# Down weights of the narrow experts in two 4 KB runs per partition, in a one-core graph network and mixture-of-experts kernel

## The chip, the cores and the metric

The kernel runs on one core of one Trainium2 chip. Its time is the device time of one execution in microseconds (us); the number that counts is the median of several. Weights lie in the chip's memory (HBM) and are copied by 16 DMA engines into SBUF, a memory of 128 partitions; TensorE (PE in the profile) multiplies from SBUF into PSUM; ScalarE (ACT) and VectorE (DVE) work between PSUM and SBUF; GpSimd (POOL) issues the gathers and scatters, SyncE (SP) the weight loads.

## The reference, cut to what matters

Two parts follow each other. The first is a graph layer on 625 rows of 512 (a segment sum over 10,625 edges, two matrix products with batch norms); it ends in x. The second is a mixture of 64 routed and 2 shared experts on the same 625 rows:

```python
x = layernorm(x)                                 # 625 x 512, one row per token
for e in range(2):                               # shared experts, all tokens
    shared += silu(x @ sWg[e]) * (x @ sWu[e]) @ sWd[e]
probs = softmax(x @ Wr)                          # 625 x 64
top_w, top_i = top_k(probs, 6)                   # six experts per token, renormalised
for e in range(64):                              # routed experts
    routed += silu(x @ Wg[e]) * (x @ Wu[e]) @ Wd[e] * gate[:, e:e+1]
out = x + shared + routed
```

Everything is float32. Each of Wg[e], Wu[e] and Wd[e] is 512 x 512, so 1 MB, and an expert has 3 MB. The kernel does not run all tokens through every expert: it gathers the rows that chose an expert, computes on those, and adds the results back by index.

## The kernel before

Up to about 200 us the graph layer runs. Then come the 64 experts, one after the other, in an order sorted by how many rows chose them (the first six are taken as they come). `CAPS` gives each position j in that order its number of slots: 96 for the first 22 positions, 64 (`BIG`) for the other 42. A position with 96 slots does its products in two pieces, 64 + 32; one with 64 slots has the first piece only. Rows beyond the slots would go through a loop at the end, whose count is read from the routing.

**Weights.** SP walks through a list `items`: gate and up weights of position j, then the down weights of position j-1. Load i goes to buffer i modulo 13 (`ring`, which in the profile has the names ring, w and ring_x, since five of the buffers share their place with earlier tensors). Before load i SP waits until the product that used the load 13 places earlier is done, reads the expert's number and issues a DMA of 1 MB. The gate and up weights are laid out "(p k)": partition p holds rows 4p to 4p+3, which are 8 KB in one piece of memory. The down weights are laid out "(k p)": partition p holds rows p, 128+p, 256+p and 384+p, which are four pieces of 2 KB.

**Products.** `tiled` (L1274) makes a product of a 64-slot position with 8 weight tiles: four slices k of the 512 rows, and for each the left and the right half of the 512 columns. The left half of the columns goes to PSUM partitions 0 to 63 and the right half to partitions 64 to 127, 256 columns each. So partition (h, token) of the gate product, column c, is feature 256h + c. `silu` (L578, ACT) turns bank 0 of PSUM into `hs`; `mult` (L941, DVE) multiplies it by the gate value and by the up product in bank 1. `h_transpose` (L1290) turns the two blocks of 128 columns of `hs`; block b then has, at partition p, features 128b + p of both halves, that is rows 256h + 128b + p of the down weights, which is slice k = 2h + b. `h_copy` moves it to `hTj`, `down` (L1298) multiplies with the down weights, `y_copy` moves the result to `ysb`, and GpSimd adds it to `out_tab` in HBM by index.

**Order on TensorE**, written out by hand, for position j: gate product of j; transposes of `hs` of j-1; transposes of the gathered rows of j+1; the small index product of j+4; up product of j; at every second position from 15 to 61 one piece of a shared expert (`unit`); down product of j-1. ACT does silu of j, the copy of `hTj` of j-1, the copy of `xT` of j+1, its part of the shared piece, and `y_copy` of j-1. DVE does the indices of j+4, the one-hot of j+6, `mult` of j and its part of the shared piece.

**Tail.** When the last scatters have landed, SP loads the two halves of `out_tab`, DVE adds them to x, and SP writes the result out.

Of the kernel before, what the change touches and what calls it, by code (L numbers as in the profile page):

```python
# [16 lines left out]
ALU = mybir.AluOpType  # L17
ACT = mybir.ActivationFunctionType
# [3 lines left out]
def gnn_moe_kernel(nc, x_in, src_in, dst_in, eps_in, W1, b1, g1, be1, W2, b2, g2, be2,  # L22
# [19 lines left out]
    BIG, SMALL = 64, 32  # L42
    CAP = BIG + SMALL
    AW = D // 2
# [5 lines left out]
    NR = 13  # L50
# [4 lines left out]
    CAPS = [CAP] * NBIG + [BIG] * (E - NBIG)  # L55
# [5 lines left out]
    with ctx:  # L61
# [129 lines left out]
        hs = [rWin.place(f"hs{i}", [128, HW], f32) for i in range(2)]  # L191
# [10 lines left out]
        ring = [rOh.place(f"ring{i}", [128, KD, 512], f32) for i in range(8)]  # L202
# [20 lines left out]
        ps = ctx.enter_context(nc.psum_tensor("ps", [128, 8, 512], f32))  # L223
# [4 lines left out]
        def sem(name):  # L228
            return ctx.enter_context(nc.semaphore(name))
# [6 lines left out]
        s_ring = [sem(f"ring_in{i}") for i in range(NR)]  # L236
# [26 lines left out]
        s_silu, s_mul, s_hc, s_y = (sem(n) for n in ("silu_done", "h_done", "hT_copied", "y_ready"))  # L263
# [14 lines left out]
        shared.append(sWd.rearrange("e (k p) n -> e p k n", p=128))  # L278
        experts = [w.rearrange("e (p k) n -> e p k n", p=128) for w in (Wg, Wu)]
        experts.append(Wd.rearrange("e (k p) n -> e p k n", p=128))  # L280

        items = []
        for j in range(E):
# [20 lines left out]
        @block.sync  # L304
        def _(sp):
            sp.dma_start(dst_i[:], dst_in.rearrange("(c p) -> c p", p=P)).then_inc(s_edges, 16)
            sp.dma_start(src_i[:], src_in.rearrange("(c p) -> c p", p=P)).then_inc(s_edges, 16)
            sp.dma_start(x_sb[:], x_in.rearrange("(t p) d -> p t d", p=P)).then_inc(s_x, 16)

            for i in range(2):  # L310
                sp.dma_start(w1[i][:], w1_of[i]).then_inc(s_w1[i], 16)
            sp.wait_ge(s_adj, T)
            for i in range(2):
                sp.dma_start(w2[i][:], w2_of[i]).then_inc(s_w2[i], 16)
            for r in range(3):
                sp.dma_start(sw[r][:], shared[r][0]).then_inc(s_sw[r], 16)
            done = (s_g, s_u, s_d)
            number = {j: j for j in range(FIXED)}
            for i, (r, j) in enumerate(items):
                if i == 8:  # L320
                    sp.wait_ge(s_z, KH)
                if i == 10:
                    sp.wait_ge(s_z, KH + KD)
                if i == 12:
                    sp.wait_ge(s_acc, 1)
                    sp.wait_ge(s_xnp, T)
                    sp.wait_ge(s_xtab, 16)
                if i >= NR:
                    r0, j0 = items[i - NR]
                    sp.wait_ge(done[r0], j0 + 1)  # L330
                if j not in number:
                    if j == FIXED:
                        sp.wait_ge(s_sorted, 1)
                    number[j] = sp.value_load(order[0:1, j:j + 1], min_val=0, max_val=E - 1)
                sp.dma_start(ring[i % NR][:], experts[r][number[j]]).then_inc(s_ring[i % NR], 16)

            sp.wait_ge(s_ov, 1)
            total = sp.value_load(ovrow[0:1, 2 * MAXOV:2 * MAXOV + 1], min_val=0, max_val=MAXOV)
            with sp.If(total > 0):
                with sp.Fori(0, total) as o:  # L340
                    e = sp.value_load(ovrow[0:1, bass.ds(o + MAXOV, 1)], min_val=0, max_val=E - 1)
                    sp.wait_ge(s_d, o + E)
                    for r in range(3):
                        sp.dma_start(ring[r][:], experts[r][e]).then_inc(s_ring[r], 16)

            sp.wait_ge(s_sy, NS * T)
            sp.wait_ge(s_scat[0], total * 16 + 8 * E)
            sp.dma_start(sums[0][:], out_tab[0][0:N, :].rearrange("(t p) d -> p t d", p=P)).then_inc(s_sum0, 16)
            sp.wait_ge(s_scat[1], 8 * E)
            for t in range(T):  # L350
                sp.dma_start(sums[1][:, t, :], out_tab[1][t * P:(t + 1) * P, :]).then_inc(s_sum1[t], 16)  # L351
            for t in range(T):
                sp.wait_ge(s_fin, t + 1)
                sp.dma_start(out[t * P:(t + 1) * P, :], x_sb[:, t, :]).then_inc(s_out, 16)
            sp.wait_ge(s_out, 16 * T)
# [90 lines left out]
        def _(act):  # L446
            sc = nc.scalar
# [68 lines left out]
            for d in range(KD):  # L516
                i = KH + d
# [60 lines left out]
            def silu(j, h, wide):  # L578
                act.wait_ge(s_g, j + 1)
                if not isinstance(j, int) or j >= 2:  # L580
                    act.wait_ge(s_th, j - 1)
                sc.activation(hs[h][:, 0:wide], ps[:, 0, 0:wide], ACT.Silu).then_inc(s_silu, 1)  # L582

            def h_copy(j, wide):
                act.wait_ge(s_th, j + 1)
# [22 lines left out]
            for j in range(E):  # L608
                silu(j, j % 2, WIDE[j])
                if j >= 1:  # L610
                    h_copy(j - 1, WIDE[j - 1])
                if j + 1 < E:
                    x_copy(j + 1, (j + 1) % 2, CAPS[j + 1])
                if j in unit_at:
                    unit(*unit_at[j])
                if j >= 1:
                    y_copy(j - 1, (j - 1) % 2, (j - 1) // 2, CAPS[j - 1])
# [4 lines left out]
            with act.If(total > 0):  # L622
                with act.Fori(0, total) as o:
                    x_copy(o + E, 0, CAP)
                    silu(o + E, 0, AW)
                    h_copy(o + E, AW)
                    y_copy(o + E, 0, o + E // 2, BIG)
# [3 lines left out]
        def _(dve):  # L631
            v = nc.vector
# [308 lines left out]
            def mult(j, h, ga, gb, wide):  # L941
                dve.wait_ge(s_silu, j + 1)
                dve.wait_ge(s_u, j + 1)
                last = v.scalar_tensor_tensor(hs[h][:, 0:AW], hs[h][:, 0:AW], ga, ps[:, 1, 0:AW], ALU.mult, ALU.mult)  # L944
                if wide > AW:
                    last = v.scalar_tensor_tensor(hs[h][:, AW:wide], hs[h][:, AW:wide], gb, ps[:, 1, AW:wide],
                                                  ALU.mult, ALU.mult)
                last.then_inc(s_mul, 1)
# [30 lines left out]
            for j in range(E):  # L979
                if j + AHEAD < E:  # L980
                    indices(j + AHEAD)
                if j + AHEAD + 2 < E:
                    slot_onehot(j + AHEAD + 2)
                mult(j, j % 2, gates[:, j, 0:1], gates[:, j, 1:2], WIDE[j])
                if j in unit_at:
                    unit(*unit_at[j])
                if j == 3:
                    extra_tiles()
                if j == 5:
                    extra_rows()  # L990
            total = dve.value_load(ovrow[0:1, 2 * MAXOV:2 * MAXOV + 1], min_val=0, max_val=MAXOV)
            with dve.If(total > 0):
                with dve.Fori(0, total) as o:
                    e = dve.value_load(ovrow[0:1, bass.ds(o, 1)], min_val=0, max_val=E - 1)
# [422 lines left out]
```

## Time and profile before

| | us |
|---|---|
| median of 3 runs | 872.74 |
| lowest, highest | 871.55, 873.14 |
| the profiled execution's own time | 871.14 |
| its span in the profile | 869.4 |
| TensorE busy | 778.0 (89%) |
| VectorE busy | 275.7 (32%) |
| ScalarE busy | 200.0 (23%) |
| GpSimd busy | 175.5 (20%) |

The span is what the profile shows from its first to its last instruction. The share of the DMA engines and the rate in GB/s are given by stretch of the span. A weight load is one instruction of SP, and its bytes move as packets on queue q1; the gathers and scatters go through q0. Of 71,518 packets 54,542 are under 8 KB. SP's instructions stand as SPq: their duration is the time until the DMA is handed over, not until it has landed.

### The profile page before, as it was taken

The page shows a single profiled execution, that of the slowest core. Times are in us where ns is not written, and L with a number is a line of the kernel's source. Part 1 is how long each engine was busy: PE and PEld are TensorE (multiplying, and loading weights), DVE is VectorE, ACT ScalarE, POOL GpSimd, SP SyncE. Part 2 cuts the span into 40 slices and gives each one's busy share as a digit, 9 for nine tenths or more (in the row PEclk, how much of TensorE's full clock was granted, in tenths as well). Part 3 has the DMA queues.
Part 4 walks back from the last instruction along what each step waited for, and adds up shares of the span by engine and source line. Part 5 has one row for each costly group of instructions (what it writes and reads, how often), then busy time and mean ns, then how long its engine had stood idle before and what let it go on. Part 6 is the DMA issues. An engine that isn't in the chain of part 4 may idle for free. (4 is left out here: it accounts for less than half of the span.)

```text
span 869.4 us, 18070 instructions
## 1 busy us (share of the span) xinstructions
PE 778.0 (89%) x7224; PEld 523.2 (60%) x7224; DVE 275.7 (32%) x833; ACT 200.0 (23%) x506; POOL 175.5 (20%) x155
## 2 busy tenths in 40 slices
PE   0789999959798999999999999999999999999920
PEld 0466877747566676666666666656666666555510
DVE  7875054366625223222111222221221121221002
ACT  0020132223022333232323222212222222122200
POOL 4000000000322233322111323222222232222110
PEclk9999999967699999999999999999999999999975
DMA  6200882032299999998988999999999999999943
GB/s 220 92 1 1 305 324 97 1 105 99 85 318 302 338 365 373 359 359 282 302 286 278 372 374 381 366 373 380 378 366 374 374 382 374 373 375 383 393 123 121
DMA packets 71518, 242.43 MB, mean 279 GB/s; under 512 B 7749, under 2 KB 7913, under 8 KB 54542
## 3 DMA queue, kind: packets, MB, share of 16 engines
q1 hardware_dynamic: 57892, 213.88, 66.0%
q0 software_dynamic: 12512, 24.12, 11.2%
q10 hardware_dynamic: 1034, 3.30, 1.0%
q8 instruction: 58, 0.95, 0.4%
q14 instruction: 22, 0.18, 0.1%
HBM read 225.72 MB, written 15.54 MB: 278 GB/s over the span
## 5 line engine op out<-in xcount | busy, mean ns | idle before, releaser
L417 POOL DMA_INDIRECT out_tab<-ysb,idx_sb x64 | 92.2, 1440 | 370.6 <-ACT ysb L593 219.2
L1278 PE MATMUL ps<-ring,xT 128*64 128x256 f32 x1296 | 158.4, 387 | 2.9 <-DMA ring<-in_L_ffn_Wu 1.1
L1278 PEld LDWEIGHTS ps<-ring,xT 128*64 128x64 f32 x1296 | 89.6, 138 | 46.6 <-issue 8.0
L899 DVE TENSOR_REDUCE gates<-ps 128x1 f32<-128x3 f32 (+1 forms) x64 | 10.3, 161 | 286.9 <-PE ps L1215 286.9
L592 ACT ACTIVATE ysb<-ps 64x256 f32<-64x256 f32 x64 | 24.1, 377 | 306.7 <-PE ps L1278 184.9
L406 POOL DMA_INDIRECT xg<-x_tab,idx_sb x64 | 70.9, 1108 | 111.7 <-DVE idx_sb L905 65.3
L1278 PE MATMUL ps<-ring,hTj 128*64 128x256 f32 x624 | 75.2, 383 | 0.0
L1278 PE MATMUL ps<-w,xT 128*64 128x256 f32 x608 | 73.4, 383 | 1.3 <-DMA w<-in_L_ffn_Wu 1.3
L861 DVE TENSOR_TENSOR onehot<-iotaAB,slotv 125x640 bf16<-125x640 f32 (+1 forms) x64 | 66.9, 1045 | 0.7
L1278 PEld LDWEIGHTS ps<-ring,hTj 128*64 128x64 f32 x624 | 42.6, 137 | 29.3 <-issue 10.4
L944 DVE SCALAR_TENSOR_TENSOR hs<-hs,gates,ps 128x256 f32<-128x256 f32 x64 | 30.7, 480 | 86.1 <-PE ps L1278 58.3
L1278 PEld LDWEIGHTS ps<-w,xT 128*64 128x64 f32 x608 | 41.7, 137 | 21.2 <-issue 3.0
L1069 PE MATMUL ps<-oh,win 125*125 x220 | 44.9, 338 | 6.9 <-DVE win L719 5.2
L1270 PE MATMUL ps<-ident,xg 64*128 64x64 f32 (+1 forms) x256 | 43.0, 289 | 0.5 <-DVE gid L845 0.5
L582 ACT ACTIVATE hs<-ps 128x256 f32<-128x256 f32 (+1 forms) x64 | 26.9, 420 | 71.3 <-PE ps L1278 40.0
L1069 PEld LDWEIGHTS ps<-oh,win 125*125 x220 | 29.0, 145 | 23.2 <-issue 13.9
L1242 PE MATMUL ps<-xnT,sw 128*128 128x312 f32 (+1 forms) x128 | 40.1, 458 | 0.4 <-ACT lg L536 0.4
L1270 PEld LDWEIGHTS ps<-ident,xg 64*128 64x128 f32 (+1 forms) x256 | 35.7, 210 | 7.8 <-issue 7.0
L1278 PE MATMUL ps<-w,hTj 128*64 128x256 f32 x320 | 38.7, 384 | 1.4 <-ACT hTj L586 1.0
L396 POOL DMA_DIRECT2D x_tab<-xn x1 | 1.7, 1669 | 178.9 <-DVE xn L743 178.9
L1250 PE MATMUL ps<-xnT,sw 128*128 128x312 f32 (+1 forms) x128 | 36.6, 428 | 0.7 <-DVE hsT L957 0.7
L1261 PE MATMUL ps<-sw,hsT 128*125 128x512 f32 x80 | 37.0, 605 | 0.0
(257 smaller groups left out, 923.2 us busy)
## 6 DMA issues: line engine op xcount, KB each, us to landing
ring<-in_L_ffn_Wg SPq DMA_DIRECT2D x41, 1024.0 KB, 18.6
ring<-in_L_ffn_Wu SPq DMA_DIRECT2D x40, 1024.0 KB, 19.3
ring<-in_L_ffn_Wd SPq DMA_DIRECT2D x39, 1024.0 KB, 20.0
w<-in_L_ffn_Wd SPq DMA_DIRECT2D x20, 1024.0 KB, 20.3
w<-in_L_ffn_Wg SPq DMA_DIRECT2D x19, 1024.0 KB, 11.4
w<-in_L_ffn_Wu SPq DMA_DIRECT2D x19, 1024.0 KB, 19.3
ring_x<-in_L_ffn_Wu SPq DMA_DIRECT2D x5, 1024.0 KB, 14.8
ring_x<-in_L_ffn_Wd SPq DMA_DIRECT2D x5, 1024.0 KB, 18.8
```

What stands on the lines that cost most here:

```text
L406: g.indirect_dma_start(out=xg[j % NX][0:CAPS[j], :], out_offset=None, in_=x_tab, in_offset=bass.IndirectOffsetOnAxis(ap=idx_sb[0:CAPS[j], ...
L417: g.indirect_dma_start(out=out_tab[h], out_offset=bass.IndirectOffsetOnAxis(ap=idx_sb[0:CAPS[j], j:j + 1].bitcast(u32), axis=0), in_=ysb[h ...
L582: sc.activation(hs[h][:, 0:wide], ps[:, 0, 0:wide], ACT.Silu).then_inc(s_silu, 1)
L592: sc.activation(ysb[h][0:BIG, 0:AW], ps[0:BIG, 3, 0:AW], ACT.Copy)
L861: v.tensor_tensor(onehot[e % 2][:].rearrange("p t a c -> p t (a c)")[:, :, 0:n], iotaAB[0:P, :, :].rearrange("p a c -> p (a c)")[:, 0:n].u ...
L944: last = v.scalar_tensor_tensor(hs[h][:, 0:AW], hs[h][:, 0:AW], ga, ps[:, 1, 0:AW], ALU.mult, ALU.mult)
L1069: t_.matmul(o, win[:, i * U + u, :], oh[:, c, c0:c1], start=False, stop=False)
L1242: last = t_.matmul(ps[:, 5, 0:PART[h]], sw[0][:, k, f * 128:(f + 1) * 128], xnT[:, k, c0:c0 + PART[h]], start=(k == 0), stop=(k == KD - 1))
L1250: last = t_.matmul(ps[:, 6, 0:PART[h]], sw[1][:, k, f * 128:(f + 1) * 128], xnT[:, k, c0:c0 + PART[h]], start=(k == 0), stop=(k == KD - 1))
L1261: last = t_.matmul(ps[0:P, 5, :], hsT[:, k, t * P:(t + 1) * P], sw[2][:, k, :], start=(k == 0), stop=(k == KD - 1))
L1270: last = t_.transpose(ps[:, 4, k * rows:(k + 1) * rows], xg[h][0:rows, :].rearrange("p (c k) -> p k c", k=KD)[:, k, :], ident[0:rows, 0:rows])
L1278: last = t_.matmul(ps[h * BIG:(h + 1) * BIG, bank, 0:AW], big(k), w[:, k, h * AW:(h + 1) * AW], start=(k == 0), stop=(k == KD - 1))
```

## The change

It concerns the 42 positions with 64 slots, and the loop for rows beyond the slots. Partition p of their down weights now holds rows 2p and 2p+1 of the upper 256 rows and rows 256+2p and 256+2p+1 of the lower ones: two pieces of 4 KB. For the transposed `hs` to fit, block b must hold the features 256h + 2p + b. So silu and the multiplication read PSUM in steps of two columns: first the even columns, which go to the first 128 columns of `hs`, then the odd ones, which go to the second 128. The bytes loaded, the transposes, the products and all waits are as before. The 22 positions with 96 slots keep the old layout throughout.

```diff
         experts.append(Wd.rearrange("e (k p) n -> e p k n", p=128))
+        down_pairs = Wd.rearrange("e (h p b) n -> e p h b n", h=2, b=2)
...
-                sp.dma_start(ring[i % NR][:], experts[r][number[j]]).then_inc(s_ring[i % NR], 16)
+                if r == 2 and CAPS[j] == BIG:
+                    sp.dma_start(ring[i % NR][:].rearrange("p (h b) n -> p h b n", h=2),
+                                 down_pairs[number[j]]).then_inc(s_ring[i % NR], 16)
+                else:
+                    sp.dma_start(ring[i % NR][:], experts[r][number[j]]).then_inc(s_ring[i % NR], 16)
...
-                    for r in range(3):
+                    for r in range(2):
                         sp.dma_start(ring[r][:], experts[r][e]).then_inc(s_ring[r], 16)
+                    sp.dma_start(ring[2][:].rearrange("p (h b) n -> p h b n", h=2), down_pairs[e]).then_inc(s_ring[2], 16)
...
-                sc.activation(hs[h][:, 0:wide], ps[:, 0, 0:wide], ACT.Silu).then_inc(s_silu, 1)
+                o, i = hs[h][:, 0:wide], ps[:, 0, 0:wide]
+                if wide == AW:
+                    o, i = o.rearrange("p (b c) -> p b c", b=2), i.rearrange("p (c b) -> p b c", b=2)
+                sc.activation(o, i, ACT.Silu).then_inc(s_silu, 1)
...
-                last = v.scalar_tensor_tensor(hs[h][:, 0:AW], hs[h][:, 0:AW], ga, ps[:, 1, 0:AW], ALU.mult, ALU.mult)
+                o, u = hs[h][:, 0:AW], ps[:, 1, 0:AW]
+                if wide == AW:
+                    o, u = o.rearrange("p (b c) -> p b c", b=2), u.rearrange("p (c b) -> p b c", b=2)
+                last = v.scalar_tensor_tensor(o, o, ga, u, ALU.mult, ALU.mult)
```

## Rows read from the trace of the kernel before

**Rows 1.** The page: span, and the DMA queue of the weight loads.
```profile
span 869.4 us, 18070 instructions
q1 hardware_dynamic: 57892, 213.88, 66.0%
```

**Rows 2.** Windows: stretch, length; busy by engine (count); clock, DMA share, GB/s.
```profile
400.00:500.00 100.00, 100.00 (x1203) 66.86 (x1200) 19.35 (x58) 27.48 (x78) 22.33 (x19) 1.00 0.93 311
600.00:700.00 100.00, 100.00 (x758) 65.07 (x758) 20.50 (x62) 23.30 (x61) 26.02 (x22) 1.00 1.03 374
740.00:785.00 45.00, 43.46 (x315) 25.38 (x311) 9.30 (x27) 9.42 (x25) 11.67 (x10) 1.00 1.04 377
785.00:828.00 43.00, 40.76 (x301) 24.27 (x297) 4.25 (x11) 9.05 (x24) 9.00 (x7) 1.00 1.03 383
```

**Rows 3.** Waits of the SP queue, 500 to 600, then 600 to 700 us.
```profile
SPq L334 <- PE ps L1278: 30.5, 11, 5.9
...
SPq L335 <- PE ps L1278: 2.0, 3, 1.1
```

**Rows 4.** Waits of TensorE, 700 to 835 us: us in total, times, longest.
```profile
PE ps L1278 <- DMA w<-in_L_ffn_Wu: 1.3, 2, 0.9
PE ps L1278 <- DMA ring<-in_L_ffn_Wu: 1.1, 2, 0.6
PE ps L1278 <- DMA ring<-in_L_ffn_Wg: 1.1, 3, 0.6
PE ps L1278 <- ACT hTj L586: 1.0, 1, 1.0
PE ps L1278 <- DMA w<-in_L_ffn_Wd: 0.5, 1, 0.5
```

**Rows 5.** DMA issues in 500 to 800 us: the down weights.
```profile
ring<-in_L_ffn_Wd SPq DMA_DIRECT2D x20, 1024.0 KB, 22.5
...
w<-in_L_ffn_Wd SPq DMA_DIRECT2D x9, 1024.0 KB, 22.8
...
ring_x<-in_L_ffn_Wd SPq DMA_DIRECT2D x3, 1024.0 KB, 21.8
```

**Rows 6.** Windows in which the weight queue runs alone (columns as in rows 2).
```profile
98.00:102.00 4.00, 3.23 (x29) 3.07 (x29) 0.00 (x0) 0.59 (x1) 0.00 (x0) 1.00 1.02 428
107.00:114.00 7.00, 7.00 (x27) 5.06 (x28) 1.29 (x5) 0.99 (x2) 0.00 (x0) 1.00 1.02 419
103.00:105.00 2.00, 2.00 (x21) 2.00 (x20) 0.00 (x0) 0.00 (x0) 0.00 (x0) 1.00 1.04 391
124.00:125.00 1.00, 1.00 (x5) 0.71 (x4) 0.00 (x0) 0.79 (x2) 0.00 (x0) 1.00 1.03 383
```

**Rows 7.** Timeline, one 64-slot position: start, us, instruction.
```profile
642.79 0.38 ACT L582 ACTIVATE hs<-ps 128x256 f32<-128x256 f32 x1 [0.96 <-PE ps L1278]
643.15 0.38 ACT L586 ACTIVATE hTj<-ps 128x256 f32<-128x256 f32 x1
...
645.65 1.90 PE L1278 MATMUL ps<-w,hTj 128*64 128x256 f32 x16
645.94 0.48 DVE L944 SCALAR_TENSOR_TENSOR hs<-hs,gates,ps 128x256 f32<-128x256 f32 x1 [0.81 <-PE ps L1278]
...
649.21 0.44 PE L1295 MATMUL ps<-ident,hs 128*128 128x128 f32 x2
```

**Rows 8.** Timeline of the last position and its scatter.
```profile
827.91 0.48 DVE L944 SCALAR_TENSOR_TENSOR hs<-hs,gates,ps 128x256 f32<-128x256 f32 x1 [5.91 <-PE ps L1278]
828.29 1.95 PE L1278 MATMUL ps<-w,hTj 128*64 128x256 f32 x16 [0.49 <-DMA w<-in_L_ffn_Wd]
...
830.17 0.44 PE L1295 MATMUL ps<-ident,hs 128*128 128x128 f32 x2
...
836.62 1.42 POOL L417 DMA_INDIRECT out_tab<-ysb,idx_sb  x1 [3.35 <-issue]
```

**Rows 9.** Groups of DVE, 195 to 225 us: a strided and a contiguous operation of 320 elements.
```profile
L844 DVE CAST gid<-lg 125x320 bf16<-125x320 f32 x1 | 1.1, 1051 | 0.0
...
L837 DVE TENSOR_TENSOR gate<-gate,rsum 125x320 f32<-125x320 f32 x1 | 0.5, 491 | 0.0
```

## The prediction

> **What bounds the kernel now.** I read the windows first, then the waits of SP and of TensorE, then the timeline at the end. The windows show two full resources at once. From 600 to 700 us TensorE is busy for all 100 us at the full granted clock, 2.4 GHz, and the DMA engines are full too: share 1.03, 374 GB/s [rows 2]. A busy TensorE can still be fed late, so the waits decide. Between 500 and 600 us SP, which issues the weight loads, still waits for TensorE to give buffers back: 30.5 us at one line alone. Between 600 and 700 it waits 2.0 us at its largest row [rows 3]. So the ring is full up to about 600 us and TensorE sets the pace; afterwards SP only waits for its queue and DMA sets it, while TensorE lives on what has already landed. About 740 us that is used up: in 740 to 785 TensorE is idle for 45.00 - 43.46 = 1.54 us, in 785 to 828 for 43.00 - 40.76 = 2.24 us [rows 2]. The waits name the cause: 1.3 + 1.1 + 1.1 + 0.5 = 4.0 us from 700 to 835 are for weights to land (gate, up and once down weights), and 1.0 us is for a copy on ACT [rows 4]. The two windows give 3.78 of it, and the rest lies just behind 828 us. No earlier product of the 64-slot positions waits on a weight load, so 4.0 us is all that faster loads can give back on TensorE.
>
> What follows TensorE is a chain in series: last product, `y_copy`, the last scatter at 836.62 [rows 8], its landing, the load of the sums, the output. It shifts with TensorE's end and the change touches none of it.
>
> **The down loads.** Each of the 42 moves the same 1.0486 MB, as 256 runs of 4 KB and not 512 of 2 KB. The price of a run's length can be read where the weight queue runs alone, at 93 to 126 us. The order of issue is known from the code (two loads of W2, shared gate, up, down, two pairs of gate and up, a down, a pair, a down), and at about 2.5 us each the stretches can be told apart. The layouts with 8 KB runs go at 428 and 419 GB/s, those with 2 KB runs at 391 and 383 [rows 6], the DMA share being 1.02 to 1.04 in all. With 420 and 390 a load takes 2.50 and 2.69 us, 0.19 apart. No row shows 4 KB loads. If each run has a fixed cost beside its bytes, four runs per partition against one cost 0.19 us, and two against one 0.06, so the change saves 0.13 us per load. The ends are 0 (the rate beside gathers and scatters is set by something else than runs) and 0.19 (4 KB is as good as 8). I take 0.13, which lies between the two rates that the trace has.
>
> From 500 to 800 us 20 + 9 + 3 = 32 down loads are issued [rows 5], all of them for 64-slot positions. In all of that time the DMA engines are full, and what they save stays in the ring as a lead. 32 x 0.13 = 4.2 us, against 4.0 us of stalls. It also comes early enough: at the first stalls, about 745 us, some 26 loads have saved 3.4 us, and the stalls up to 785 us are 1.5. At 400 to 500 us the share is 0.93 with 311 GB/s [rows 2], the engines are not full, and I count nothing there. So all stalls on weights go: -4.0 us. It is close: at 0.09 per load instead of 0.13 the lead is 2.9 us and stalls of 1.1 us stay.
>
> The Trainium skill speaks against this term. In "DMA: Bandwidth & Descriptors", Specifications, a transfer has its full line rate from 512 B up; by that rule 2 KB runs lose nothing, the saving is 0 and the time stays at 872.7. The alone-running stretches disagree, with 391 against 419 to 428 GB/s, and I go by them; this rule gets its chance as rival 1.
>
> SP's side: the number of load instructions and their waits are the same. Fewer runs can only shorten the hand-over of a load to the queue; TensorE does not wait for SP. POOL's queue, with the gathers and scatters, is not moved, and it has the same packets. Its packets take turns with longer ones, which I estimate at under 1 us per scatter, and a scatter's buffer is needed only two positions later, over 13 us away.
>
> **The reads in steps of two.** 42 silus (0.38 us each) and 42 multiplications (0.48) read PSUM every second word [rows 7]. No row shows such a read from PSUM. From below it is free; from above stands a DVE operation with steps, 320 elements in 1051 ns against 491 without [rows 9], a factor of 2.1, so +0.4 us on silu and +0.5 on the multiplication. I take 0, since the 1051 row also writes two-byte numbers ten bytes apart and nothing here does. Either way it is covered. Behind silu on ACT stands the copy of `hTj`, which ends at 643.53; the down product that needs it starts its multiplications at 645.65, so there are about 1.9 us (PE loads its first weights about 0.2 us before). Behind `mult`, which ends at 646.42, come the transposes at 649.21: 2.8 us [rows 7]. ACT's next copy, of `xT`, would be late by what silu grew, and is needed only at the next gate product, about 3 us later. At the very end cover is thinnest: the last `mult` ends at 828.39, the transposes start at 830.17, and 0.49 us of that distance is a stall that I expect to go [rows 8]: 1.3 us of cover against 0.5. Cost 0. Once the two together exceeded their cover by x, 42 positions would pay 42x.
>
> The Trainium skill has a rule here too, in "SBUF — State Buffer", the note on cachelines: PSUM has lines of two float32 values, and a pattern that is not contiguous slows matmuls. Only ACT and DVE read PSUM here. If the same held for them and every read took twice as long, the additions of 0.38 and 0.48 us would lie under the same cover and the sum would not change.
>
> **Sum.** Profiled execution: 871.14 - 4.0 = 867.1 us (the span 869.4 becomes 865.4). The median of the runs shown lies 1.6 us above that execution, so 872.74 - 4.0 = 868.7 us. The 1.0 us wait for `hTj` stays: ACT is then at the `y_copy` of the position before, in the same order as now.
>
> **Rivals.**
> 1. *The packet length does not count in a loaded queue.* 374 to 383 GB/s with scatters in between [rows 2] is well under both lone rates, so memory or the turns with q0 may be what limits; weights on q1 have 66.0% of the engines' time over the span [rows 1], and all else would have to fill in. Then a Wd load lands when it did, and the stalls stay: 872.7. Against it: the share is above 1 in both, so the engines themselves are the full resource. Also here: the run of two rows is cut back into rows when the DMA is built, and the change does not do what it says. The 8 KB layout, whose four rows move faster than four separate rows, speaks against that. Together 0.20.
> 2. *Half of it.* The saving is about 0.07 per load, 32 x 0.07 = 2.2 us of lead, the last stalls stay: 872.7 - 2.2 = 870.5, on the edge of what can be told. 0.15.
> 3. *Slower: 4 KB runs 512 KB apart move worse than 2 KB runs 256 KB apart*, for example because the 16 engines then meet in the same part of the memory. Place: the queue from 500 us on, in the ring's lead. It decides as soon as a down load is longer at all, as TensorE already stalls at the end; every 0.1 us per load gives 32 x 0.1 = 3.2 us, so 876 us. For it speaks only that the pattern is new; against it that the 8 KB layout, with larger steps from partition to partition, is the fastest of the trace. 0.06.
> 4. *Slower: the reads outgrow their cover*, beyond 1.9 us for silu. Nothing in the rows comes near (the ends are 0.4 and 0.5). 0.02.
>
> The forecast itself has 0.57. What differs from these cases by accident of the runs is small: two medians of this kernel can be told apart at about 0.2%, 1.75 us, so faster means under 871.0 and slower over 874.5. The forecast and two thirds of rival 2 are faster: 0.57 + 0.10 = 0.67, and rounding in a small possibility of more at the tail (the last scatters meet fewer weight packets) 0.68. Same: rival 1 and the rest of rival 2, 0.25. Slower: 0.07. The range starts at 866.8, 1.9 us under the forecast, for a saving of 0.19 per load with a shorter tail, and ends at 873.0, above rival 1.
>
> **What would show it.** Right: in the changed kernel TensorE's waits for weights after 700 us are gone or under 0.5 us; q1 has some 42 x 256 = 10,752 packets fewer than 57,892 and less than 66.0% of the engines; SP waits for TensorE (buffers) beyond 600 us; the last down product ends about 4 us earlier and the tail behind it has its old length; silu and `mult` stay at 0.38 and 0.48 us. Wrong: the packets are as many as before (not done), or fewer with the share as before (rival 1); stalls that are more (rival 3); TensorE waiting for `hs` or `hTj` in mid-stage (rival 4).

## The result: 866.65 us, half a per cent faster

The changed kernel takes 866.65 us (median of 6 runs, 864.33 to 868.56); the kernel before, run beside it, 871.65 us (6 runs, 869.87 to 873.14). The ratio is 0.9942 with a 95% interval of 0.9925 to 0.9958. That is 5.0 us less where 4.0 were forecast, and the interval, 3.7 to 6.5 us, holds the forecast. The time itself lies 2 us under the forecast 868.7 and 0.15 us under the lower end of the range, 866.8.

The page of the changed kernel, beside [rows 1]:

```profile
span 866.8 us, 18070 instructions
q1 hardware_dynamic: 47140, 213.88, 65.4%
```

The weight queue has 57,892 - 47,140 = 10,752 packets fewer, as 42 loads of 256 instead of 512 give, for the same bytes. Its share is smaller: 0.660 x 869.4 = 573.8 us per engine before, 0.654 x 866.8 = 566.9 after, 6.9 us or 0.16 us per changed load. The same reading in two more executions with 4 KB runs (e1 and e2 below) gives 0.20 and 0.22, so it is good to some 0.05 us.

Windows of the changed kernel, beside [rows 2]:

```profile
600.00:700.00 100.00, 100.00 (x755) 64.96 (x753) 21.17 (x65) 23.38 (x62) 26.03 (x23) 1.00 1.03 383
740.00:785.00 45.00, 45.00 (x330) 26.36 (x332) 10.18 (x30) 10.19 (x28) 12.80 (x11) 1.00 1.03 378
785.00:825.00 40.00, 40.00 (x301) 23.69 (x299) 4.39 (x13) 9.06 (x25) 9.01 (x7) 1.00 1.01 385
```

With the DMA engines as full as before, 383 GB/s pass from 600 to 700 us instead of 374 (from 500 to 800 us it is 381 instead of 375), and TensorE has no idle time in the two stretches in which it had 1.54 and 2.24 us.

The waits of TensorE, 700 to 835 us, beside [rows 4], and one row of SP's waits from 600 to 700 us, beside [rows 3]:

```profile
PE ps L1290 <- ACT hTj L595: 1.0, 1, 1.0
PE ps L1290 <- DMA w<-in_L_ffn_Wd: 0.2, 1, 0.2
...
SPq L335 <- PE ps L1290: 14.3, 9, 2.8
```

The waits for gate and up weights are gone and one of 0.2 us for the last but one down weights is left; SP is again waiting for TensorE in a stretch in which it waited for its queue alone.

The end of the stage in the changed kernel, beside [rows 8]:

```profile
825.56 0.48 DVE L956 SCALAR_TENSOR_TENSOR hs<-hs,gates,ps 128x256 f32<-128x256 f32 x1 [5.22 <-PE ps L1290]
825.61 1.95 PE L1290 MATMUL ps<-w,hTj 128*64 128x256 f32 x16 [0.17 <-DMA w<-in_L_ffn_Wd]
827.49 0.44 PE L1307 MATMUL ps<-ident,hs 128*128 128x128 f32 x2
...
828.88 1.95 PE L1290 MATMUL ps<-w,hTj 128*64 128x256 f32 x16 [0.96 <-ACT hTj L595]
...
833.94 1.42 POOL L423 DMA_INDIRECT out_tab<-ysb,idx_sb  x1 [3.35 <-issue]
```

**Where the two profiled executions differ.** They are only 871.14 - 868.56 = 2.6 us apart. The multiplications on VectorE are a clock for the whole stage, since they start at the same rhythm in both. Here is position 11, first before, then after:

```profile
348.76 0.48 DVE L944 SCALAR_TENSOR_TENSOR hs<-hs,gates,ps 128x256 f32<-128x256 f32 x1 [0.88 <-PE ps L1283]
```

```profile
351.00 0.48 DVE L956 SCALAR_TENSOR_TENSOR hs<-hs,gates,ps 128x256 f32<-128x256 f32 x1 [0.88 <-PE ps L1295]
```

At this point the changed kernel is 2.24 us late, in work that the change does not touch. Most of it is there early. VectorE, idle before this comparison of the graph layer, starts it 1.61 us later, and the profile names no engine or transfer that it waits for. First before, then after:

```profile
22.94 3.09 DVE L719 TENSOR_TENSOR win<-iota,dcol 125x1375 int16 x2 [3.45 <-issue]
```

```profile
24.55 3.09 DVE L728 TENSOR_TENSOR win<-iota,dcol 125x1375 int16 x2 [5.05 <-issue]
```

In the twelve executions of the experiments this gap was 2.94 to 5.19 us, so it varies by itself. By 212 us some 0.5 us of the distance has come back, and another 1.2 us is added in a window in which the granted clock was 0.83 and not 0.91, before and then after:

```profile
270.00:290.00 20.00, 17.67 (x268) 12.33 (x262) 8.21 (x30) 4.62 (x12) 5.91 (x4) 0.91 0.88 297
```

```profile
270.00:290.00 20.00, 17.67 (x236) 12.21 (x234) 7.72 (x34) 5.63 (x16) 4.40 (x3) 0.83 0.83 278
```

An index product near its start begins at 271.69 before and at 272.74 after, 1.05 us later; a product near its middle begins at 281.58 and 283.82, 2.24 us later. TensorE was longer at the lower of its two levels (1.2 and 2.4 GHz). The last down product before the change starts here:

```profile
831.56 1.95 PE L1278 MATMUL ps<-w,hTj 128*64 128x256 f32 x16 [0.95 <-ACT hTj L586]
```

From position 11 to the last multiplication the rhythm gives 827.91 - 348.76 = 479.15 us before and 825.56 - 351.00 = 474.56 after, 4.59 less; to the start of the last down product 831.56 - 348.76 = 482.80 and 828.88 - 351.00 = 477.88, 4.92 less. Read so, the profile agrees with the 5.0 us of the runs. From that product to the last scatter it is 5.06 us in both, so the tail moved along unchanged.

### The profile page after: what moved, and what is told of

It is laid out like the page before. It is cut to its first block and busy times, and to the rows that moved or that the text cites. A ratio compares the mean times of both kernels' runs of the same rounds, so it can differ in the third digit from the quotient of the medians.

```text
span 866.8 us, 18070 instructions
## 1 busy us (share of the span) xinstructions
PE 777.1 (90%) x7224; PEld 522.1 (60%) x7224; DVE 275.4 (32%) x833; ACT 200.2 (23%) x506; POOL 175.6 (20%) x155
## 3 DMA queue, kind: packets, MB, share of 16 engines
q1 hardware_dynamic: 47140, 213.88, 65.4%
```

## The experiments

Each ratio is against the kernel before, run on the same chip beside it. "Rhythm" is the time from the multiplication of position 11 to that of position 63 in the profile: 479.15 us before, 474.56 after the change.

**e1: the changed kernel once more.**

> The changed kernel once more, beside the kernel before on one chip. Theory (lead in the ring: shorter down loads take away TensorE's waits for weights at the end of the expert stage): 4.6 us under before, by the starts of the multiplications on VectorE in the two traces (-2.24 us of distance at position 53, +2.35 at position 63), so a ratio of 0.9947. Rival (part of the 5.0 us measured is the graph layer's clock in the runs that happened to be drawn): the ratio comes out nearer to 1, 0.996 or more, here.

Measured: 867.41 us, ratio 0.9938 (0.9923 to 0.9954), 5.4 us less. The gain repeats, and is not smaller. Its profiled execution had 0.7 us of waits for weights, 0.2 and 0.5 us before the last up and the last but one down product, where the first one had 0.17. Its rhythm is 474.81 us, 4.34 less than before.

**e2: 4 KB runs alone; e3: stepped reads alone.** Each takes the other half of the change away:

```diff
 e2, in silu and in mult
-                if wide == AW:
-                    o, i = o.rearrange("p (b c) -> p b c", b=2), i.rearrange("p (c b) -> p b c", b=2)
 e3
-                if r == 2 and CAPS[j] == BIG:
+                if False:
```

> The 4 KB runs without the reads in steps of two (the pairing of features and weight rows is left out). Theory: the same time as e1 within 0.5 us, no wait of TensorE for gate or up weights. Rival (the stepped reads cost or bring something): it differs from e1 by over 1 us.

> The reads in steps of two on the old layout of 2 KB runs (the pairing of features and weight rows is left out). Theory: as before within 1 us, TensorE's waits for weights in the last 100 us of the stage some 4 us as before, silu 383 ns and multiplication 480 ns. Rival (the reads take part in the gain or cost): off from before by over 1.5 us.

Measured: e2 867.79 us, ratio 0.9945 (0.9930 to 0.9960), rhythm 474.56 us; e3 872.08 us, ratio 1.0000 (0.9987 to 1.0012), rhythm 479.0 us, with 1.3 us of waits at its largest row, for gate weights. Up to the intervals, of some 1.3 us each way, all of the gain is in the load and the stepped reads cost nothing. ACT and DVE took as long in the changed kernel as before, where the medians are 383 and 480 ns (operation, shortest, median and longest in ns, where the longest of ACT is the 384-column form):

```profile
L591 ACT ACTIVATE hs<-ps x64: 384/384/492, 234.7 to 823.2; 128x256 f32<-128x256 f32 x42, 128x384 f32<-128x384 f32 x22
...
L956 DVE SCALAR_TENSOR_TENSOR hs<-hs,gates,ps x64: 479/480/483, 239.7 to 825.6; 128x256 f32<-128x256 f32 x64
```

**e4: half of the down weights left out.**

```diff
-                    sp.dma_start(ring[i % NR][:].rearrange("p (h b) n -> p h b n", h=2),
-                                 down_pairs[number[j]]).then_inc(s_ring[i % NR], 16)
+                    sp.dma_start(ring[i % NR][:, 0:2, :], down_pairs[number[j]][:, 0]).then_inc(s_ring[i % NR], 16)
```

> The 64-slot positions load only the first half of their down weights (256 rows, one 4 KB run per partition; the other half is left out), 0.5 MB or 1.25 us of DMA less per position. It asks whether the changed kernel is at the floor that TensorE sets. Theory: all waits for weights are gone already but for 0.2 us, so it is at most 0.5 us under e1. Rival (DMA still limits somewhere in the changed kernel, for example before position 22 or by slowing other transfers): 2 us or more under e1.

Measured: 866.58 us, ratio 0.9935 (0.9921 to 0.9948); no wait for weights at all. Its multiplications of positions 11 and 63:

```profile
349.76 0.48 DVE L955 SCALAR_TENSOR_TENSOR hs<-hs,gates,ps 128x256 f32<-128x256 f32 x1 [0.88 <-PE ps L1294]
...
824.32 0.48 DVE L955 SCALAR_TENSOR_TENSOR hs<-hs,gates,ps 128x256 f32<-128x256 f32 x1 [5.22 <-PE ps L1289]
```

824.32 - 349.76 = 474.56 us, the rhythm of the changed kernel to the hundredth. So up to this multiplication the change reaches the floor that TensorE sets, and 4.59 us is what the waits had cost until then. Behind it a little is left. The last down product of e4 starts here:

```profile
827.25 1.95 PE L1289 MATMUL ps<-w,hTj 128*64 128x256 f32 x16 [0.96 <-ACT hTj L594]
```

That is 827.25 - 349.76 = 477.49 us after position 11, where it is 482.80 before and 477.88 after the change. In all the waits for weights had cost 5.3 us, of which the change takes away 4.9.

**e5: 8 KB runs for the down weights.** The load takes the "(p k)" view of the gate weights.

> All 64-slot positions load their down weights in one 8 KB run per partition, as gate and up (the pairing of features and weight rows is left out; the same bytes). Theory: each load is another 0.06 us shorter, but nothing waits for it any more: same time as e1 within 0.5 us. q1's share falls further, to about 65.0%, and SP waits longer for TensorE. Rival (the run length still pays): 1.5 us or more under e1.

Measured: 867.16 us, ratio 0.9947 (0.9931 to 0.9964), rhythm 474.56 us again. q1's share is 64.9%, where e1 has 65.2%, and SP waits far more for buffers: 42.5 us at its largest row from 600 to 700 us, where the changed kernel has 14.3. The loads did become shorter, and all that was left to gain from it was 0.4 us at the last products (829.11 - 351.61 = 477.50 us to the last down product).

**e6 and e7: 4 KB runs for half of the positions.**

```diff
-                if r == 2 and CAPS[j] == BIG:
+                if r == 2 and CAPS[j] == BIG and j < 43:      (e6; e7 has j >= 43)
```

> 4 KB runs for the down weights of positions 22 to 42 only, 2 KB runs for 43 to 63 (the pairing is left out for the latter). Theory: the ring carries a lead over, so time saved from about 480 us on still counts at 745 us; some 16 of these 21 loads fall in the stretch with full DMA engines, 16 x 0.13 = 2.1 us, so about 2.1 us under before (0.9976). Rival (only loads near the stalls count): as before.

> 4 KB runs for positions 43 to 63 only, 2 KB runs for 22 to 42 (the pairing is left out for those). Theory: 21 x 0.13 = 2.7 us of lead, so about 2.7 us under before (0.9969) and stalls of about 1.9 us left in TensorE's waits; at 0.16 per load 3.4 us. Rival (only loads near the stalls count): as e1, 4.6 us under before.

Measured: e6 869.01 us, ratio 0.9963 (0.9947 to 0.9979); e7 869.03 us, ratio 0.9969 (0.9953 to 0.9986). The times do not tell them apart (3.2 and 2.7 us under before by the ratios, each within 1.5), the rhythm does: e6 476.84 us, 2.3 saved; e7 475.99, 3.2 saved. e6's waits, 0.7 us each for gate and up weights and less for others, all come after 785 us, while its last 4 KB load was issued at 619.29 us, over 160 us before. So time saved early is carried along in the ring: the rival, that only late loads count, fails on both. In e7 all 21 loads lie where the engines are full, which gives a direct price. The up product of position 63, which the last multiplication follows, waits for its weights in both kernels, first before, then e7:

```profile
825.85 1.95 PE L1278 MATMUL ps<-ring,xT 128*64 128x256 f32 x16 [0.63 <-DMA ring<-in_L_ffn_Wu]
```

```profile
822.86 1.95 PE L1290 MATMUL ps<-ring,xT 128*64 128x256 f32 x16 [0.43 <-DMA ring<-in_L_ffn_Wu]
```

In the order of the list, the down weights of positions 62 and 63 come behind these up weights. So 19 of the 21 changed loads stand before them, and a down load in two runs per partition costs 3.16 / 19 = 0.17 us less than one in four (0.16 with e3's 479.0 us in place of before's rhythm). At that price e6's 2.31 us are 14 loads; I had counted 16.

**e8: gate and up weights in 2 KB runs, on the kernel before.**

> The kernel before with the gate and up weights of the 64-slot positions in four 2 KB runs instead of one of 8 KB (the pairing with the gathered rows is left out; the same bytes). It prices the run length with a large dose. Theory (each run has a fixed cost in a loaded queue too): 0.19 us more per load, 0.38 per position, over the some 36 positions with full DMA engines 13.7 us slower, and a little more since the lead is gone earlier: 884 to 889 us. Rival (in the loaded queue memory or the turns with the other queue set the rate): as before within 2 us.

Measured: 882.2 us, ratio 1.0124 (1.0099 to 1.0149), slower by 10.8 us by the ratio and 10.0 by the rhythm (489.18 us). The direction and the place are the theory's, with 4.6 us of waits at the largest row, for gate weights, but the size is three quarters of it: with the 36 positions that I had counted 10.0 / 72 = 0.14 us per load, where 0.19 was expected; e6's 14 loads of 21 would put the beginning at position 29 and give 70 loads, again 0.14. The median lies under the range I had given. DMA engines at share 1.06 moved 364 GB/s from 600 to 700 us:

```profile
600.00:700.00 100.00, 98.49 (x737) 64.24 (x735) 19.35 (x58) 23.23 (x61) 25.90 (x22) 1.00 1.06 364
```

**e9: 8 KB runs with the right pairing.** Other than in e5, nothing is left out here. To allow it, the two halves of PSUM take other columns in the gate and up products:

```diff
+                        if quads:
+                            cols = w[:, k, :].rearrange("p (g h b) -> p h g b", h=2, b=2)[:, h]
```

> 8 KB runs for the down weights with the right pairing: the gate and up products of the 64-slot positions take columns 4g, 4g+1 for one half of PSUM and 4g+2, 4g+3 for the other (the moving operand is read in pairs, 16 bytes apart), so that with the stepped reads of the change partition g holds features 4g to 4g+3 and the down weights can lie as the gate weights do. Theory (the changed kernel is at TensorE's floor): same time as e1 and e5, 867 us or ratio 0.994, if TensorE reads pairs at full pace; 16 matmuls of a product stay at 1.9 us. Rival (a read that is not contiguous slows the product): the product takes longer, and every 0.1 us of it is 84 x 0.1 = 8.4 us, so slower than before from 0.06 us on.

Measured: 873.7 us, ratio 1.0030 (1.0019 to 1.0042), about 8 us behind e1 by the two ratios. The rival wins, and the 8 KB loads are not the reason, since e5 has them without the loss. In e9 a gate and an up product take 1.98 and 2.04 us from first to last of their 16 matmuls (1.90 and 1.95 in the changed kernel), the down product behind them, with its old columns, 1.91:

```profile
644.37 1.98 PE L1292 MATMUL ps<-w,xT 128*64 128x256 f32 x16
...
647.48 2.04 PE L1292 MATMUL ps<-w,xT 128*64 128x256 f32 x16
649.34 1.91 PE L1292 MATMUL ps<-w,hTj 128*64 128x256 f32 x16
```

0.085 x 84 = 7.1 us; the rhythm grew by 481.80 - 474.56 = 7.24.

**e10 to e12: work of TensorE moved behind the last product,** to see how much lead the ring has left. One or two 3.7 us pieces of the second shared expert go there, and the first sums' buffer moves to the ring's place:

```diff
+        unit_at = {15 + 2 * i: u for i, u in enumerate(units[GAP:len(units) - TAIL])}
+        late_units = units[len(units) - TAIL:]
...
             down(E - 1, weights(2, E - 1), WIDE[E - 1])
+            for u in late_units:
+                unit(*u)
```

> The changed kernel with the last piece of the second shared expert (3.7 us of TensorE) moved behind the last down product, where TensorE is otherwise idle, and the first sums' buffer moved to the ring so that it can be loaded meanwhile. It asks how much lead the 4 KB runs leave over. Theory (e6 and e7 together saved 5.5 us of landing time where 4.6 was needed): TensorE wants 3.7 us more, 0.9 of it is there, so about 0.9 us under e1 and some 2.8 us of waits for weights are back. Rival (no DMA limit is left in the changed kernel): 3.7 us under e1.

> e9 and the moved piece together. Theory: 8 KB runs save another 0.06 us in each of some 36 loads, 2.3 us, beside the 0.9 left over: 3.2 of the 3.7 us can be had, so 863 to 864 us, ratio 0.990 to 0.991, with at most 0.6 us of waits for weights. Rival (the sums or the tail take the time back, or the pairs slow TensorE): no better than e1.

> As e11 with the last two pieces behind the last down product. Theory: the lead is used up by the first piece, so the waits for weights grow by about 3.7 us and the time is that of e11 within 1 us. Rival (TensorE alone sets the time): another 3.7 us under e11.

Measured: e10 865.62 us, ratio 0.9940 (0.9927 to 0.9953), no better than e1. Its waits for weights are back:

```profile
PE ps L1297 <- DMA ring<-in_L_ffn_Wg: 2.1, 2, 1.2
...
PE ps L1297 <- DMA w<-in_L_ffn_Wd: 0.5, 1, 0.5
PE ps L1297 <- DMA ring<-in_L_ffn_Wd: 0.4, 1, 0.4
PE ps L1297 <- DMA ring<-in_L_ffn_Wu: 0.2, 1, 0.2
```

From its position 11 (349.25 us) to its last multiplication (823.76) it is 474.51 us, although 3.7 us of TensorE's work are gone from between: the lead that the 4 KB runs leave over is nearly nothing, not the 0.9 us expected. Its up product of position 63 starts at 821.70 - 349.25 = 472.45 us, where it is 825.85 - 348.76 = 477.09 before: all the 4 KB loads together bring these weights 4.6 us earlier, not the 2.3 + 3.2 = 5.5 of e6 and e7. Where the other 0.8 us went was not separated. The changed kernel stands at both limits at once.

e11 gave 870.40 us, ratio 0.9989 (0.9976 to 1.0002), and e12 867.09 us, 0.9954 (0.9941 to 0.9967). Both times are wrong for my theory, and the rivals hold. With 8 KB runs and e9's slower products, which give DMA 7 us more, neither has a wait for weights, and each piece moved is worth its full price (rhythm of e9 481.80, of e11 478.03, of e12 474.25: 3.77 and 3.78 less). The ratios fall by 0.0041 and 0.0035, 3.6 and 3.1 us. The tail thus hides two pieces, and the slower products cost more than these bring. None of the twelve is measurably better than the change itself.

## Where the prediction was wrong, and what in it was right

The time came out under the range. The mechanism held, but two terms of the sum were off: what the stalls cost was put too low, and the starting point of 872.74 us was too high. The price per load was too low as well.


- *Which resource ends last* was right: TensorE paces the stage up to about 740 us, then it waits for weights (e4 takes just these waits away and gets the same rhythm as the change). The wait rows of the changed kernel fell to 0.2 us as I had said; in e1 they were 0.7, over the 0.5 that I had given as a sign.
- *The stalls, 4.0 us,* is the step that failed: I took the summed wait rows as "all that faster loads can give back on TensorE". Against e4 the stalls cost 4.6 us up to the last multiplication and 5.3 to the start of the last down product, and the change took 4.9 of these away (4.35 in e1's execution). A wait also breaks the overlap of one product with the next, and no wait row carries that. Before the change the down product starts at 786.18 and the gate product, which waits for weights, at 788.30:

```profile
786.18 1.90 PE L1278 MATMUL ps<-ring,hTj 128*64 128x256 f32 x16
788.30 1.95 PE L1278 MATMUL ps<-ring,xT 128*64 128x256 f32 x16 [0.23 <-DMA ring<-in_L_ffn_Wg]
```

```profile
786.52 1.90 PE L1290 MATMUL ps<-ring,hTj 128*64 128x256 f32 x16
788.25 1.90 PE L1290 MATMUL ps<-ring,xT 128*64 128x256 f32 x16
```

  The second fence is the changed kernel. From start to start it is 2.12 us with the wait and 1.73 without, 0.39 us, of which the row shows 0.23. The rest is the overlap: without the wait the gate product starts 0.17 us before the modelled end of the down product (786.52 + 1.90 = 788.42). The same comparison of starts at each of the eight waits gives 0.16 to 0.18 us beyond the row at the three gate products, 0.07 or 0.08 at the four up products and nothing at the down product. About 0.05 us more is lost at the transposes behind each gate product, and 0.15 before one up product that has no wait row at all. With 0.17 us of wait left in the changed kernel, its rows account for 3.8 of the 4.9 us, and these pieces for the other 1.1.
- *The price,* 0.13 us per load, was too low: 0.16 to 0.17 by e7, 0.16 to 0.22 by q1's share. This and the stalls go together: at 0.13 the forecast lead of 4.2 us could not have paid for the 4.9 us that came back. The lead was enough, but by e10 with next to nothing over.
- *The stepped reads cost nothing:* right, and more so than I had argued. I covered up to 0.5 us each; there was nothing to cover (e3). The rule of the Trainium skill on PSUM's lines ("SBUF — State Buffer", cachelines) speaks of matmuls; in ACT and DVE, with one step of two float32 values, no such cost is seen. e9 shows 4% on TensorE, but for a moving operand in SBUF, where the same note lets float32 step up to 16 bytes for free.
- *Rival 1,* with the Trainium skill's line rate from 512 B up ("DMA: Bandwidth & Descriptors", Specifications), is excluded: e2 has the gain with nothing changed but the runs, and e8 makes the gate and up runs 2 KB and loses 10 us at full DMA engines. *Rival 2* (half of it) saves 2.2 us, and the interval begins at 3.7. *Rivals 3 and 4* did not occur.
- *The scale,* 872.74 us, was a median of 3. The kernel before has since had medians of 871.65 (6 runs), 872.08 (17), 871.86 (26) and 870.82 (23), single runs from 867.58 to 874.06. Of the 2.05 us between forecast and result, 1.1 is this and 1.0 the gain. My range went 1.9 us below the forecast, less than these two together: its lower end took in a better price per load, but neither a lower base nor a larger sum of stalls. That three runs had a median 1.1 us high is accident, not mechanism; without it the time would have been inside the range.

**Open.** Two runs fewer per partition saved 0.17 us per load (e7), three more cost 0.14 (e8). A fixed cost per run would make these 0.17 and 0.25. The time of q1's packets did grow by about that: 0.675 x 880.5 = 594.3 us per engine in e8 against 573.8, over 84 loads 0.24 us each. Why only 0.14 of it reached the kernel's time is not shown.

## What to carry to other kernels

When two resources are full at once, ask from which point on the one that feeds is late, and read the sum of stalls as start-to-start differences of a regular instruction, not from the wait rows: here these showed 4.0 of 5.3 us. A saving per transfer then counts from the moment at which the transfers run without a gap, as long as a deep ring can carry it; beyond what the stalls cost it is worth nothing. And put a new order on the engine with slack: a stepped read was free here on ACT and DVE, and a stepped read of TensorE's moving operand cost 7 to 8 us.

## What the runs showed of the hardware

- With the DMA engines full, from 500 to 800 us at share 1.04 and 1.03, the same loads passed at 375 GB/s with a third of the weights in 2 KB runs and at 381 GB/s with that third in 4 KB runs. Per load of 1 MB that was 0.16 to 0.17 us (e7).
- Silu and the multiplication, 128 x 256 float32, took 383 or 384 ns and 480 ns, whether they read PSUM column by column or every second one.
- A matmul whose moving operand, 256 float32, was read from SBUF in pairs 16 bytes apart took 391 ns instead of 382 on average, and a product of 16 of them 1.98 to 2.04 us instead of 1.90 to 1.95.
- Unchanged code up to position 11 differed by 2.24 us between two executions. An idle gap of VectorE was 5.05 us instead of 3.45, and 1.2 us was added from 271 to 282 us, in a stretch of 20 us with the granted clock at 0.83 instead of 0.91.
- A wait of 0.23 us of TensorE moved the next product by 0.39 us, since without it that product starts 0.17 us before the end of the one before.
